# The order of the first loads and of the first TensorE work in a conditioned residual kernel

## Chip, cores and metric

The kernel runs on one core of one Trainium2 chip. The metric is the device time of one execution in microseconds (us); lower is better. A profiled execution gives the span from its first to its last instruction, and the time of the run lies a little above that span.

## What is computed

The batch has 128 samples, each a 128 x 1024 matrix of float32. Every sample picks one of 200 matrices for the first layer and one of 8 matrices and bias rows for the second.

```python
def _L0_cond_ref(x, conditions, weights):
    w = weights[conditions]
    return jnp.einsum('bct,bcd->bdt', x, w)

def _L1_cond_ref(x, subjects, weights, bias):
    w = weights[subjects]
    b = bias[subjects]
    out = jnp.einsum('bct,bcd->bdt', x, w)
    out = out + b[:, :, None]
    return out
x = x + _L0_cond_ref(x, itok_B_1_198, L0_cond_weights)
x = x + _L1_cond_ref(x, itok_B_0_7, L1_cond_weights, fside_8xS_0)
```

## The kernel before, in words

Both layers are folded into one matrix for each sample. With J = W1 + I (`j_all`, made once on VectorE at L348), the output is (W0 J + J) applied to x, plus the bias. So for each sample TensorE makes the 128 x 128 product W0 J (L291, in `product`), VectorE adds J to it and leaves M in `m_sb` (L374, in `sum_m`), and TensorE multiplies M with the two halves of x (L310, in `results`). VectorE takes the left half out of PSUM with the bias (L382), ScalarE the right half (L406), both in place into the x tile `xy`.

Samples go in pairs (1 MB of x), two pairs make a quad (2 MB), and `xy` holds a ring of eight pairs, four quads, so the 64 pairs take eight rounds. All large transfers are issued from SyncE (SP) in one written order: loads of x by pair (`load_pair`, L151) or by quad (`load_quad`, L148), loads of w0 of 64 KB for each sample (`load_one`, L129), and stores by pair (L166) or by quad (L162). A slot of the ring is loaded again only when its store has landed (L170). Transfers are issued in program order, and a wait on SP holds back everything behind it.

The w0 matrices stay in SBUF (`w0_home`), one place for each sample. In the first round every sample's matrix is loaded. From the second round on a sample whose matrix is already there skips its load; for this a table of homes is worked out in the prologue. TensorE spreads the 128 condition words over partitions (L316, L317), VectorE compares them in four steps (L353 to L360, each raises `home_step`), TensorE turns the resulting column into a row (L324, raises `home_turned`), and VectorE writes `load_words` and `pick_words` from it (L365, L367; four steps raise `home_ready`). SP waits for `home_ready` before the first load of the second round (L187), and GpSimd (POOL) before its picks of the second round (L272).

In the prologue SP issues `j_all` (L176), the two first pairs of x (L178, L179), waits for the condition words (L180, loaded from ScalarE's queue at L409), and then issues four w0 loads for each quad, with the next quad of x between them (L181 to L184). `load_w0_first` first reads four words into registers (L123) and then issues four transfers (L129). TensorE's queue holds the first product (L321), the turn of the table (L324), and then the alternation of results and products. The first product waits for the first pair's w0 (L285), and for POOL's copies of J (`picked`, L256, L258). VectorE's queue holds, in this order, the four comparing steps, two copies of words (L362, L363), the wait for `home_turned` (L364) with L365 and L367 behind it, and then the first sum (L386).

Of the kernel before, what the change touches and what calls it, by code (L numbers as in the profile page):

```python
# [11 lines left out]
def conditioned_residual_kernel(nc, x, cond, w0_t, w1_bias, out):  # L12
# [11 lines left out]
    NQ, C, QB, T = x.shape  # L24
    B = NQ * QB
    N0, _, D = w0_t.shape
    N1 = w1_bias.shape[1]
    assert C == D == 128
    PAIR = 2
    RING = 8  # L30
    QUAD = QB // PAIR
    QUADS = RING // QUAD
# [11 lines left out]
    with ExitStack() as ctx:  # L44
# [3 lines left out]
        def sem(name):  # L48
            return ctx.enter_context(nc.semaphore(name))
# [35 lines left out]
        pair_loaded = [sem(f"pair_loaded{s}") for s in range(QUAD)]  # L85
# [15 lines left out]
        def half(h):  # L101
            return slice(h * HALF, (h + 1) * HALF)

        def slots(q):
            return xy[:, q * QUAD:(q + 1) * QUAD, :, :].rearrange("c s k t -> c (s k t)")

        def quad_of(t, r, q):
            return t[bass.ds(r * QUADS + q, 1), :, :, :].rearrange("n c k t -> (n c) (k t)")

        def pair_of(t, n, s):  # L110
            return t[n, :, (s % QUAD) * PAIR:(s % QUAD + 1) * PAIR, :].rearrange("c k t -> c (k t)")
# [8 lines left out]
        def _(sp):  # L120
# [12 lines left out]
            def load_w0_first(q):  # L133
                words = words_of(cond_words[0:1, 0, q * QB:(q + 1) * QB])
                for k in range(QB):
                    load_one(q * QB + k, q * QUAD + k // PAIR, words[k], None)
# [10 lines left out]
            def load_quad(r, q):  # L147
                sp.dma_start(slots(q), quad_of(x, r, q)).then_inc(x_loaded[q], 16)  # L148

            def load_pair(n, s, loaded):  # L150
                sp.dma_start(xy[:, s, :, :].rearrange("c k t -> c (k t)"), pair_of(x, n, s)).then_inc(loaded, 16)  # L151
# [21 lines left out]
            def load_w0_of(r, q):  # L173
# [1 line left out]

            sp.dma_start(j_all[:].rearrange("c n d -> c (n d)"), w1_bias.rearrange("c n d -> c (n d)"))\  # L176
              .then_inc(w1_loaded, 16)
            for s in range(QUAD):  # L178
                load_pair(0, s, pair_loaded[s])  # L179
            sp.wait_ge(cond_loaded, 16)  # L180
            for q in range(QUADS):  # L181
                load_w0_first(q)
                if q < QUADS - 1:
                    load_quad(0, q + 1)  # L184


            sp.wait_ge(home_ready, 4)  # L187
# [42 lines left out]
        def _(pool):  # L230
            def pick(r, s):


                pool.wait_ge(w0_loaded[s], r * (PAIR * 16) + PAIR * 16)
                _, words = nc.values_load_multi_w_load_instructions(
                    pick_words[0:1, bass.ds(r * ROUND_B + s * PAIR, PAIR), :].rearrange("o b f -> o (b f)"),
                    engines=(mybir.EngineType.Pool,),
                    skip_runtime_bounds_check_because="each word is checked against its own range below")
                for k in range(PAIR):
                    home = nc.s_assert_within(words[2 * k], 0, B - 1)  # L240
                    i = nc.s_assert_within(words[2 * k + 1], 0, N1 - 1)
                    nc.gpsimd.tensor_copy(w0_pick[:, s, k, :],  # L242
                                          w0_home[:, bass.ds(home, 1), :].rearrange("k b c -> k (b c)"))
                    last = nc.gpsimd.tensor_copy(  # L244
                        j_pick[:, s, k, :], j_all[:, bass.ds(i, 1), :].rearrange("c n d -> c (n d)"))
                last.then_inc(picked, 1)

            def pick_first(s):


                _, words = nc.values_load_multi_w_load_instructions(
                    cond_words[0:1, 1, s * PAIR:(s + 1) * PAIR], engines=(mybir.EngineType.Pool,),
                    skip_runtime_bounds_check_because="each word is checked against its own range below")
                for k in range(PAIR):
                    i = nc.s_assert_within(words[k], 0, N1 - 1)
                    last = nc.gpsimd.tensor_copy(  # L256
                        j_pick[:, s, k, :], j_all[:, bass.ds(i, 1), :].rearrange("c n d -> c (n d)"))
                last.then_inc(picked, 1)  # L258
# [20 lines left out]
        @block.tensor  # L279
        def _(pe):  # L280
            def product(r, s, first=False):

                pe.wait_ge(picked, r * RING + (s + 1))
                if first:
                    pe.wait_ge(w0_loaded[s], PAIR * 16)  # L285
                if not first or s >= MB:

                    pe.wait_ge(m_ready[s % MB], r * (RING // MB) + s // MB)
                for k in range(PAIR):
                    w0_of_k = w0_home[:, s * PAIR + k, :] if first else w0_pick[:, s, k, :]  # L290
                    last = nc.tensor.matmul(m_ps[:, s % MB, k * D:(k + 1) * D], w0_of_k,  # L291
                                            j_pick[:, s, k, 0:D], start=True, stop=True)
                last.then_inc(product_ready, 1)

            def results(r, s, k, first=False, last=False):

                b = s * PAIR + k
                if k == 0:
                    if first and s < QUAD:
                        pe.wait_ge(pair_loaded[s], 16)  # L300
                    elif not last:
                        pe.wait_ge(x_loaded[s // QUAD], r * 16 + (16 if s >= QUAD else 0))
                    pe.wait_ge(m_ready[s % MB], r * (RING // MB) + (s // MB + 1))
                for h in range(2):
                    if last:
                        pe.wait_ge(last_x_loaded[2 * k + h], 16)
                    if not first or b >= YB:

                        pe.wait_ge((left_out, right_out)[h][b % YB], r * (ROUND_B // YB) + b // YB)
                    nc.tensor.matmul(y_ps[:, b % YB, h, :], m_sb[:, s, k, :], xy[:, s, k, half(h)],  # L310
                                     start=True, stop=True).then_inc(y_ready, 1)


            pe.wait_ge(ones_ready, 1)
            pe.wait_ge(cond0_row_ready, 1)
            nc.tensor.matmul(cond0_ps[:, 0:B], ones[:], cond0_row[:], start=True, stop=True)  # L316
            nc.tensor.matmul(cond0_ps[:, B:B + 1], cond0_row[:], ones[0:1, 0:1], start=True, stop=True)\  # L317
              .then_inc(cond0_spread, 1)


            product(0, 0, first=True)  # L321
            pe.wait_ge(eye_ready, 1)
            pe.wait_ge(home_step, 4)
            nc.tensor.matmul(home_ps[0:1, 0:B], home_less_b[:], eye[:], start=True, stop=True)\  # L324
              .then_inc(home_turned, 1)
            for s in range(1, RING):
                results(0, s - 1, 0, first=True)
                product(0, s, first=True)
                results(0, s - 1, 1, first=True)
            with pe.Fori(1, ROUNDS) as r:  # L330
                results(r - 1, LAST, 0)
                product(r, 0)
                results(r - 1, LAST, 1)
                for s in range(1, RING):
                    results(r, s - 1, 0)
                    product(r, s)
                    results(r, s - 1, 1)
            for k in range(PAIR):
                results(ROUNDS - 1, LAST, k, last=True)
# [110 lines left out]
```

## Time and profile before

| what | value |
|---|---|
| time, median of 3 runs | 342.62 us (342.51 to 342.78) |
| time of the profiled run | 343.0 us |
| its span | 341.2 us |
| TensorE matmul busy | 272.9 us (80%) |
| VectorE, ScalarE, GpSimd busy | 126.3, 97.0, 65.8 us |
| moved by DMA | 140.80 MB, mean 413 GB/s |
| share of SP's queue (q1) in 16 DMA engines' span | 98.7% |
| mean granted TensorE clock, of full speed | 0.952 |

The profiled run took 343.0 us, of which the span is 341.2 us, so 1.8 us lie around it; it is 0.4 us above the median. In the views below, times are counted from the span's start. PE is TensorE's matmul, PEld its weight load, DVE is VectorE, ACT ScalarE, POOL GpSimd, and SPq the queue of SyncE. The share of DMA is that of 16 DMA engines together, and since packets overlap, it can stand a little above 1.

### The profile page before, as it was taken

To read this page: it belongs to the slowest core of one execution; us is meant where nothing else is said; L and a number is where in the kernel's file an instruction comes from. 1 tells how busy PE (TensorE), PEld (TensorE's weight loads), DVE (VectorE), ACT (ScalarE), POOL (GpSimd) and SP (SyncE) were. 2 spreads that over 40 slices of the span, in tenths; PEclk is the share of its full clock that TensorE was granted. 3 is DMA by queue.
4 is the path that set the end of the run, shared out by engine and by line. 5 is a ranking of instruction groups with operands and counts; after the bars stand their busy time and mean duration, and the time that the engine had idled before them with its cause. 6 is when DMAs were issued, how large, how long until landed. Compare 5 with 4: busy or idle time off the path is not lost.

```text
span 341.2 us, 4867 instructions
## 1 busy us (share of the span) xinstructions
PE 272.9 (80%) x774; PEld 131.8 (39%) x774; DVE 126.3 (37%) x202; ACT 97.0 (28%) x135; POOL 65.8 (19%) x249
## 2 busy tenths in 40 slices
PE   1799997678777798786997977889697987978980
PEld 1355443334333354343443433444343443434430
DVE  3145543343333334243442433434243432424440
ACT  1033352232322224132241324313143321323330
POOL 2400311131122211222111222121222111222000
PEclk9999999999999979799897999979799997989996
DMA  7999999999999999999999999999999999999993
GB/s 304 417 409 396 422 430 419 413 423 421 432 434 423 426 422 414 431 424 423 427 427 423 431 430 426 427 421 426 433 426 430 427 429 426 425 426 424 413 387 137
DMA packets 24058, 140.80 MB, mean 413 GB/s; under 512 B 2673, under 2 KB 14322, under 8 KB 15474
## 3 DMA queue, kind: packets, MB, share of 16 engines
q1 hardware_dynamic: 23760, 140.20, 98.7%
q10 hardware_dynamic: 290, 0.53, 0.4%
q14 instruction: 7, 0.06, 0.0%
q8 instruction: 1, 0.02, 0.0%
HBM read 76.03 MB, written 67.11 MB: 419 GB/s over the span
## 4 chain that ended last, share of the span: by engine, by line
DMA 61%; SPq 16%; PE 13%; issue 7%; ACT 0%; DVE 0%; DVEq 0%
DMA out<-xy 54%; PE y_ps L310 11%; SPq L129 9%; SPq L123 5%; DMA xy<-x 4%; DMA w_home<-w_t 2%; PE m_ps L291 2%; SPq L148 2%; ACT xy L406 0%; SPq L162 0%; SPq L151 0%; SPq L203 0%; SPq L156 0%; PE home_ps L324 0%; SPq L176 0%
## 5 line engine op out<-in xcount | busy, mean ns | idle before, releaser
L310 PE MATMUL y_ps<-xy,m_sb 128*128 128x512 f32 x512 | 251.4, 627 | 49.2 <-DMA xy<-x 48.2
L310 PEld LDWEIGHTS y_ps<-xy,m_sb 128*128 128x128 f32 x512 | 94.6, 200 | 155.1 <-issue 155.1
L406 ACT ACTIVATE xy<-y_ps,j_pick 128x512 f32<-128x512 f32 x128 | 88.0, 687 | 227.4 <-PE y_ps L310 227.4
L382 DVE TENSOR_SCALAR xy<-y_ps,j_pick 128x512 f32<-128x512 f32 x128 | 96.1, 751 | 147.9 <-PE y_ps L310 147.9
L242 POOL COPY w_pick<-w_home 128x128 f32 x112 | 33.2, 296 | 238.3 <-issue 238.3
L291 PEld LDWEIGHTS m_ps<-j_pick,w_pick 128*128 128x128 f32 x224 | 35.7, 200 | 30.2 <-issue 29.7
L374 DVE TENSOR_TENSOR m_sb<-m_ps,j_pick 128x256 f32<-128x256 f32 x64 | 27.2, 425 | 47.7 <-PE m_ps L291 46.1
L291 PE MATMUL m_ps<-j_pick,w_pick 128*128 128x128 f32 x224 | 34.9, 279 | 0.0
L244 POOL COPY j_pick<-j_all 128x129 f32 x112 | 33.4, 298 | 0.1
L291 PE MATMUL m_ps<-j_pick,w_home 128*128 128x128 f32 x32 | 5.9, 315 | 6.6 <-DMA w_home<-w_t 6.6
L406 ACT ACT_TABLE_LOAD x7 | 9.0, 1283 | 7.5 <-POOL j_pick L256 7.4
L291 PEld LDWEIGHTS m_ps<-j_pick,w_home 128*128 128x128 f32 x32 | 5.7, 225 | 10.6 <-POOL j_pick L256 7.2
L256 POOL COPY j_pick<-j_all 128x129 f32 x16 | 4.8, 298 | 9.9 <-issue 9.5
L316 PE MATMUL cond_ps<-cond_row,ones 1*128 1x128 f32 x2 | 0.8, 482 | 2.4 <-DVE cond_row L345 2.4
L365 DVE TENSOR_TENSOR load_words<-home_ps,batch_less_b 1x128 int32<-1x128 f32 x1 | 0.3, 280 | 5.0 <-PE home_ps L324 5.0
L348 DVE TENSOR_TENSOR j_all<-j_all,eye 128x1024 f32<-128x1024 f32 x1 | 1.2, 1226 | 1.9 <-DMA j_all<-w_bias 1.9
L316 PEld LDWEIGHTS cond_ps<-cond_row,ones 1*128 1x128 f32 x2 | 0.5, 305 | 2.4 <-issue 2.4
L345 DVE CAST cond_row<-cond_words 1x128 f32<-1x128 int32 x1 | 0.2, 215 | 2.1 <-DMA cond_words<-cond 2.1
L324 PE MATMUL home_ps<-eye,home_less_b 128*1 128x128 f32 x2 | 0.6, 394 | 0.0
L317 PEld LDWEIGHTS cond_ps<-ones,cond_row 1*128 1x128 f32 x2 | 0.5, 328 | 0.0
L317 PE MATMUL cond_ps<-ones,cond_row 1*128 1x1 f32 x2 | 0.4, 277 | 0.0
L355 DVE TENSOR_SCALAR same<-cond_ps,cond_col 128x128 f32<-128x128 f32 x1 | 0.4, 351 | 0.0
(16 smaller groups left out, 2.8 us busy)
## 6 DMA issues: line engine op xcount, KB each, us to landing
xy<-x SPq DMA_DIRECT2D x30, 2048.0 KB, 15.1
out<-xy SPq DMA_DIRECT2D x29, 2048.0 KB, 15.0
w_home<-w_t SPq DMA_DIRECT2D x128, 64.0 KB
out<-xy SPq DMA_DIRECT2D x5, 1024.0 KB, 9.7
xy<-x SPq DMA_DIRECT2D x3, 1024.0 KB, 7.7
xy<-x SPq DMA_DIRECT2D x4, 256.0 KB, 13.4
j_all<-w_bias SPq DMA_DIRECT2D x1, 516.0 KB, 3.4
out<-xy SPq DMA_DIRECT2D x2, 256.0 KB, 4.7
```

Of the source, the lines that this page charges most:

```text
L123: return nc.values_load_multi_w_load_instructions(words, engines=(mybir.EngineType.SP,), min_val=0, max_val=N0 - 1, skip_runtime_bounds_ch ...
L129: sp.dma_start(w0_home[:, bass.ds(b, 1), :].rearrange("k b c -> k (b c)"), w0_t[bass.ds(i, 1), :, :].rearrange("n k c -> (n k) c"), cond=n ...
L148: sp.dma_start(slots(q), quad_of(x, r, q)).then_inc(x_loaded[q], 16)
L242: nc.gpsimd.tensor_copy(w0_pick[:, s, k, :], w0_home[:, bass.ds(home, 1), :].rearrange("k b c -> k (b c)"))
L244: last = nc.gpsimd.tensor_copy(j_pick[:, s, k, :], j_all[:, bass.ds(i, 1), :].rearrange("c n d -> c (n d)"))
L256: last = nc.gpsimd.tensor_copy(j_pick[:, s, k, :], j_all[:, bass.ds(i, 1), :].rearrange("c n d -> c (n d)"))
L291: last = nc.tensor.matmul(m_ps[:, s % MB, k * D:(k + 1) * D], w0_of_k, j_pick[:, s, k, 0:D], start=True, stop=True)
L310: nc.tensor.matmul(y_ps[:, b % YB, h, :], m_sb[:, s, k, :], xy[:, s, k, half(h)], start=True, stop=True).then_inc(y_ready, 1)
L316: nc.tensor.matmul(cond0_ps[:, 0:B], ones[:], cond0_row[:], start=True, stop=True)
L374: nc.vector.tensor_tensor(m_sb[:, s, :, :], m_ps[:, s % MB, 0:PAIR * D].rearrange("c (k d) -> c k d", k=PAIR), j_pick[:, s, :, 0:D], ALU.a ...
L382: nc.vector.tensor_scalar(xy[:, s, k, half(0)], y_ps[:, b % YB, 0, :], j_pick[:, s, k, D:D + 1], None, ALU.add).then_inc(left_out[b % YB], 1)
L406: nc.scalar.activation(xy[:, s, k, half(1)], y_ps[:, b % YB, 1, :], ACT.Identity, bias=j_pick[:, s, k, D:D + 1]).then_inc(right_out[b % YB ...
```

## The change

Two orders are changed in the prologue; no instruction is added or removed.

On SP, the first four w0 loads, with the wait for the condition words and the reading of the words, are moved from behind both first pairs of x to between them. The second pair follows them. From there the order of transfers is as before: quad 1, w0 of quad 1, quad 2, w0 of quad 2, quad 3, w0 of quad 3.

On TensorE, the turn of the table of homes with its two waits is moved ahead of the first product.

```diff
--- before.py
+++ after.py
@@ -175,13 +175,13 @@
 
             sp.dma_start(j_all[:].rearrange("c n d -> c (n d)"), w1_bias.rearrange("c n d -> c (n d)"))\
               .then_inc(w1_loaded, 16)
-            for s in range(QUAD):
-                load_pair(0, s, pair_loaded[s])
+            load_pair(0, 0, pair_loaded[0])
             sp.wait_ge(cond_loaded, 16)
-            for q in range(QUADS):
+            load_w0_first(0)
+            load_pair(0, 1, pair_loaded[1])
+            for q in range(1, QUADS):
+                load_quad(0, q)
                 load_w0_first(q)
-                if q < QUADS - 1:
-                    load_quad(0, q + 1)
 
 
             sp.wait_ge(home_ready, 4)
@@ -318,11 +318,11 @@
               .then_inc(cond0_spread, 1)
 
 
-            product(0, 0, first=True)
             pe.wait_ge(eye_ready, 1)
             pe.wait_ge(home_step, 4)
             nc.tensor.matmul(home_ps[0:1, 0:B], home_less_b[:], eye[:], start=True, stop=True)\
               .then_inc(home_turned, 1)
+            product(0, 0, first=True)
             for s in range(1, RING):
                 results(0, s - 1, 0, first=True)
                 product(0, s, first=True)
```

## Rows read from the trace of the kernel before

**Rows 1.** The page, part 2: DMA share in tenths and GB/s, 40 slices

```profile
DMA  7999999999999999999999999999999999999993
GB/s 304 417 409 396 422 430 419 413 423 421 432 434 423 426 422 414 431 424 423 427 427 423 431 430 426 427 421 426 433 426 430 427 429 426 425 426 424 413 387 137
```

**Rows 2.** Busy time by stretch, later stages; the columns stand in the first line

```profile
core 0: us, PE busy (x) PEld busy (x) DVE busy (x) ACT busy (x) POOL busy (x), PEclk, DMA share, GB/s
12.00:32.00 20.00, 19.27 (x51) 9.79 (x52) 8.29 (x15) 5.50 (x8) 2.09 (x7) 1.00 1.02 401
32.00:42.00 10.00, 10.00 (x33) 5.14 (x32) 5.03 (x9) 3.44 (x5) 3.21 (x12) 1.00 1.03 429
62.00:322.00 260.00, 213.82 (x607) 102.37 (x606) 96.58 (x151) 75.54 (x106) 53.53 (x200) 0.95 1.01 426
322.00:335.00 13.00, 8.91 (x24) 3.70 (x22) 4.35 (x7) 3.74 (x6) 0.00 (x0) 1.00 0.94 385
335.00:341.00 6.00, 0.00 (x0) 0.00 (x0) 0.00 (x0) 0.00 (x0) 0.00 (x0) 0.54 0.11 43
```

**Rows 3.** The same view, the first 7 us

```profile
1.80:2.00 0.20, 0.00 (x0) 0.00 (x0) 0.00 (x0) 0.00 (x0) 0.04 (x1) 1.00 2.01 227
2.00:7.00 5.00, 0.98 (x4) 0.92 (x4) 2.70 (x8) 0.00 (x0) 0.29 (x1) 1.00 0.96 383
```

**Rows 4.** The chain of waits in order of time: start, length, what

```profile
3.44 6.46 DMA w_home<-w_t
10.04 1.19 PE m_ps L291 x4
11.23 0.53 PE home_ps L324 x2
12.73 3.75 PE y_ps L310 x4
38.91 0.70 ACT xy L406
```

**Rows 5.** Timeline of SP's queue: start, length, engine, line, operation, tiles

```profile
0.79 0.39 SPq L176 DMA_DIRECT2D j_all<-w_bias  x1
1.23 0.89 SPq L151 DMA_DIRECT2D xy<-x  x2
2.88 2.16 SPq L129 DMA_DIRECT2D w_home<-w_t  x4
5.09 0.44 SPq L148 DMA_DIRECT2D xy<-x  x1
12.93 7.04 SPq L129 DMA_DIRECT2D w_home<-w_t  x6
20.70 0.35 SPq L166 DMA_DIRECT2D out<-xy  x1
28.05 4.22 SPq L166 DMA_DIRECT2D out<-xy  x2
```

**Rows 6.** Timeline of DVE and POOL ahead of the first product

```profile
2.09 0.21 DVE L345 CAST cond_row<-cond_words 1x128 f32<-1x128 int32 x1 [2.09 <-DMA cond_words<-cond]
6.20 0.29 DVE L360 TENSOR_REDUCE home_less_b<-same_batch 128x1 f32<-128x128 f32 x1
6.65 0.66 POOL L256 COPY j_pick<-j_all 128x129 f32 x2 [4.80 <-issue]
```

**Rows 7.** Issue to landing, in order: L176; L151, both first pairs

```profile
DMA to landing us min/median/max: 3.4/3.4/3.4
DMA to landing us min/median/max: 5.7/6.7/7.7
```

**Rows 8.** Issue to landing: L166 issued at 31.9; all L148; all L162

```profile
DMA to landing us min/median/max: 7.2/7.2/7.2
DMA to landing us min/median/max: 10.2/15.1/16.3
DMA to landing us min/median/max: 10.6/15.0/17.8
```

## The prediction

> **What bounds the kernel now.** I read the page's DMA line first. The 16 DMA engines are busy for nine tenths or more of every slice from the second to the last but one, and what they move hardly varies [rows 1]. TensorE is busy for 80% of the span, but in the long middle its matmuls fill 213.8 of 260 us while the DMA share is 1.01 at 426 GB/s [rows 2]. So the candidate is DMA, and the question for a change in the prologue is whether DMA ever runs dry between the first and the last byte. If it does not, work that is done earlier elsewhere buys nothing.
>
> The second view is busy time by stretch. From 2 to 7 us the share is 0.96 [rows 3], from 12 to 42 us it is 1.02 and 1.03 [rows 2]. It is idle only before 1.8 us [rows 3], and it thins out only after 335 us: 43 GB/s from 335 to 341 us with PE, DVE and ACT at zero [rows 2]. A sixteenth of 426 is 27 GB/s, so there some one or two of the 16 DMA engines work off what is left to them while all others are done. The last 6 us are therefore DMA too, the arrears of the slowest DMA engine, and not a computation that came late.
>
> The third view is the time from issue to landing. A quad of 2.1 MB takes 2.1/0.426 = 4.9 us to move, yet a quad's load needs at least 10.2 us from its issue and 15.1 at the median, a quad's store at least 10.6 and 15.0 [rows 8]. Even the shortest had some 5 us of other transfers ahead of it. The shallowest place in round 0 is the store of pair 3: its issue is the second of the two that start at 28.05, ends at 32.3 and so starts at 31.9 [rows 5], and it lands 7.2 us later [rows 8], against 1.05/0.426 = 2.5 us of its own. A backlog of over 4 us stands there as well.
>
> The chain of waits tells another story for the first 39 us: the landing of w0 at 3.44 + 6.46 = 9.90, then the product, the turn of the table, and TensorE without a break to 38.9 us [rows 4]. TensorE is on that chain because SP's stores wait for its results. But a chain names who came last at each wait, and not whether the queue behind it was empty. The landings say that it was not.
>
> **Part 1: w0 of the first four between the pairs.** Nothing is added. What moves on SP is the wait for the condition words, the reading of words, and four issues; what they are moved past is the issue of pair 1 alone.
>
> *When the w0 arrives.* Pair 0, issued at 1.23, lands 5.7 us later at 6.9; pair 1, issued at about 1.70 (the second of the row's two), lands 7.7 us later at 9.4 [rows 5, 7]. The four w0 land 0.5 us after it, at 9.9 [rows 4]. Without pair 1 ahead of them they land at 6.9 + 0.5 = 7.4, which is 2.5 us earlier, the time of one pair (1.05 MB at some 0.42 MB/us). They are in the queue in time: their issues start at 2.88 now [rows 5], behind the end of pair 1's issue at 2.12 and the reading of words. In the new order the SP is free at 1.65, but the condition words arrive only near 2.1 (VectorE, which waits for them too, starts at 2.09 [rows 6]), so the w0 issues move by 0.1 us at most.
>
> *What that does to pair 1.* It is issued where the four w0 issues end, 2.88 + 2.16 = 5.04 [rows 5], instead of 1.70. Pair 1 lands at 7.4 + 2.5 = 9.9, the time at which pair 1 and the four w0 are both there today. Its reader, the third and fourth result, comes after 13 us by the sum below, so nobody waits. Quad 1 and all behind it are issued one pair issue (0.42 us) later than now. By 7 us DMA has taken 0.05 + 5 x 0.383 = 1.96 MB [rows 3] of the 5.0 MB then issued, so this is hidden.
>
> *Does DMA run dry at 6 us?* This is the price that the trace of before does not show. Ahead of pair 1 stand j_all (0.53 MB), pair 0 (1.05) and four w0 (0.26), 1.84 MB. At 0.383 MB/us from 2 us, with 0.05 MB before it [rows 3], they last until 2 + 1.79/0.383 = 6.7 us. The nearest row for the start of a transfer is the first one: j_all is issued at 0.79 [rows 5] and data flow at 227 GB/s from 1.8 [rows 3], 1.0 us. That puts pair 1's first data at 6.0, with 0.7 us to spare, and the price at zero. The other end: j_all lands 3.4 us after its issue [rows 7], of which 0.53/0.40 = 1.3 is moving, so all fixed time together is 2.1 us. Were all of that before the first byte, data would come at 7.1 and DMA would be idle for 0.4 us. I take zero, since the row with the first data shows the start itself, and keep 0.4 us as the upper end.
>
> A rule of the Trainium skill speaks against the change here: "DMA: Bandwidth & Descriptors", section "Anatomy of one DMA", gives about 2.0 us of fixed time for each transfer beside bytes over 436 GB/s. By it j_all would need 3.2 us, and the trace has 3.4. Put wholly ahead of the data, it would leave DMA idle for 0.3 us. The page itself places most of it behind the last byte, which would leave nothing idle.
>
> **Part 2: the turn of the table ahead of the product.** Both waits of the turn are met early: the eye comes from POOL long before, and the last step of `home_step` ends at 6.20 + 0.29 = 6.49 [rows 6]. The turn (0.53 us [rows 4]) then runs from 6.6 to 7.2, inside the wait for the w0 of 7.4. It costs the product nothing. Were the w0 to land before 6.6, the product would wait for at most 0.6 us. What goes is the turn behind the product and the two VectorE steps ahead of the first sum (L365, L367): now the product ends at 11.23 and the first result starts at 12.73 [rows 4], 1.5 us later; afterwards only the sum and its hand-over are left, some 0.6 us.
>
> **The sum on TensorE.** Product from max(w0 7.4, first picks 6.65 + 0.66 = 7.3 [rows 6], turn 7.2) + 0.14 = 7.55; 1.19 us for the product [rows 4] gives 8.7; sum and hand-over 0.6; first result at 9.3 instead of 12.73. TensorE is 3.4 us ahead and stays so until the end of round 0 (38.9 becomes 35.5). POOL's picks come in time, and no x load is late for it: quad 1 lands at 5.09 + 10.2 = 15.3 [rows 5, 8], and its first reader comes behind pairs 0 and 1: at round 0's mean of 26.2/8 = 3.3 us a pair [rows 4], not before 9.3 + 6.5 = 15.8.
>
> **What is late next.** SP. Six w0 issues, from 12.93 on, take 7.04 us [rows 5] where four take 2.16: the queue is full and accepts a transfer only as fast as DMA drains. SP reaches the first store's wait at 20.0 whatever TensorE does, and issues it at 20.70, so of the 3.4 us this store sees at most 0.7. The later stores of round 0 may be issued up to 3.4 us earlier, but behind a backlog of over 4 us. They land when the bytes ahead of them have moved, in the same order as before. The first reload of a slot waits for such a landing, not for TensorE. There the 3.4 us end. From then on the order of transfers, their bytes, the start of the first and the fullness of the queue are as before, so the end is as before: 0 us, against the profiled run 341.2 in the span and 343.0 in all. The forecast is the median of the three runs, 342.6 us.
>
> **Rivals.**
> 1. *The start is on the path after all.* The chain has TensorE from 10 to 38.9 us [rows 4]. If DMA's share near 1 hid transfers that merely wait, each earlier store would bring the next load forward, and the gain would be up to 3.4 us: 339.2 us. The 401 GB/s between 12 and 32 us against 426 later [rows 2] speak for it a little: 20 us x 25/426 = 1.2 us are lost there. Against it stand the landings [rows 8] and the many short w0 rows in that stretch. Chance 0.07. Half of the 1.2 us, 0.6, is the lower end that I allow to the forecast.
> 2. *A gap at 6 us, slower.* If pair 1's first data come later than 6.7 us, DMA stands idle, and a queue that never runs dry later cannot make it up: each 0.1 us of gap is 0.1 us at the end. It shows as slower from a gap of 0.7 us on, that is, if the first data come 2.4 us after the issue at 5.0. At 0.8 us the time is 343.4. The start of 1.0 us [rows 3, 5] speaks against it; the w0 issues at 0.54 us each, slower than DMA moves them, speak for it. Chance 0.06.
> 3. *The order does not do what it says.* The w0 may still land near 9.9, if the small transfers are held up behind something else than pair 1. Then only the turn is gained on TensorE, 0.9 us, and the time is again 342.6. Chance 0.03.
>
> **How the numbers follow.** The forecast has 0.84. About 0.2% (0.7 us) is what a measurement of this kernel can tell from no change. The forecast and rival 3 both lie within it: same 0.87. Rival 1 is faster, 0.07; rival 2 is slower, 0.06. The forecast's own bounds are 342.6 - 0.6 and 342.6 + 0.4, with 0.2 for the scatter of the runs on the upper side, and as it holds over 8 in 10, the range reaches to no other case: 342.0 to 343.2.
>
> **What the profile afterwards would show.** First product near 7.5 and first result near 9.3 us; pair 1 landing near 9.9 and quad 1 near 15.3, as before; the DMA share between 5 and 8 us near 1 (a hole there is rival 2); the first store of SP near 20; the first reload at the same time as before, within half a microsecond; TensorE through round 0 near 35.5; and the stretch 335 to 341 as it was. The prediction is wrong if the first reload comes over 1 us earlier and the span shrinks with it, or if the DMA is found dry.

## The result, and the profile after

| | before | changed |
|---|---|---|
| median of 12 runs each | 342.62 us (342.15 to 343.54) | 343.99 us (342.99 to 345.33) |
| ratio | | 1.0038, 95% interval 1.0023 to 1.0052 |
| profiled run, its span | 343.0, 341.2 us | 344.31, 342.5 us |

The change makes the kernel slower by 1.3 us, 0.38%. Two further comparisons of the same kernel gave 1.0021 (1.0007 to 1.0036) and 1.0029 (1.0019 to 1.0040), so 0.7 to 1.3 us by the ratios. The forecast was no change.

The page of the changed kernel, part 2, in the lines that answer to [rows 1]:

```profile
DMA  7999999999999999999999999999999999999985
GB/s 257 411 416 383 416 382 421 413 415 429 427 429 423 421 421 432 423 427 420 424 427 423 434 434 417 428 418 427 436 419 429 436 433 412 441 429 418 421 357 214
```

The first slice holds 257 GB/s instead of 304. The slice from 42.8 to 51.4 us is low too, 382 instead of 430. The others look much as before, up to the last two. Busy time by stretch, against [rows 2] (engines' busy us, granted clock, DMA share, GB/s):

```profile
12.00:32.00 20.00, 19.09 (x57) 9.71 (x56) 8.70 (x14) 6.18 (x9) 2.37 (x8) 1.00 1.02 398
...
42.00:52.00 10.00, 5.76 (x13) 2.53 (x12) 2.16 (x4) 2.66 (x3) 2.12 (x8) 0.83 1.01 389
...
62.00:322.00 260.00, 208.56 (x603) 100.63 (x602) 96.55 (x151) 75.12 (x105) 54.23 (x204) 0.97 1.01 425
322.00:335.00 13.00, 11.78 (x34) 5.46 (x32) 5.86 (x9) 4.81 (x7) 0.00 (x0) 1.00 0.90 379
335.00:341.00 6.00, 0.00 (x0) 0.00 (x0) 0.00 (x0) 0.00 (x0) 0.00 (x0) 0.81 0.60 229
```

The long middle is as before, 425 GB/s against 426. The last stretch now carries 229 GB/s where it had 43: bytes that were not moved earlier are moved here. They are (229 - 43) x 6 us = 1.1 MB, more than one hole at the start accounts for. Most of them belong to two stretches. One is the hole between 5.5 and 8 us, which the rest of this section and most experiments are about. The other lies at 42 to 52 us, where the kernel before has

```profile
42.00:52.00 10.00, 10.00 (x30) 4.88 (x29) 5.13 (x8) 4.72 (x6) 1.07 (x4) 1.00 1.01 422
```

There the changed kernel moves 389 GB/s, which is (422 - 389) x 10/426 = 0.8 us of transfer, and TensorE is busy for 5.76 us instead of 10, since it waits for x. It comes back in "Why the prediction was wrong". The first hole is seen in the same view in steps of half a microsecond, of the changed kernel:

```profile
5.00:5.50 0.50, 0.00 (x0) 0.00 (x0) 0.50 (x1) 0.00 (x0) 0.00 (x0) 1.00 1.04 426
5.50:6.00 0.50, 0.00 (x0) 0.00 (x0) 0.47 (x3) 0.00 (x0) 0.00 (x0) 1.00 0.81 331
6.00:6.50 0.50, 0.00 (x0) 0.00 (x0) 0.47 (x2) 0.00 (x0) 0.00 (x0) 1.00 0.83 270
6.50:7.00 0.50, 0.00 (x0) 0.00 (x0) 0.47 (x3) 0.00 (x0) 0.00 (x0) 1.00 0.60 160
7.00:7.50 0.50, 0.39 (x2) 0.11 (x2) 0.22 (x2) 0.00 (x0) 0.31 (x2) 1.00 0.51 140
7.50:8.00 0.50, 0.36 (x2) 0.17 (x2) 0.27 (x2) 0.12 (x1) 0.28 (x1) 1.00 0.95 310
8.00:8.50 0.50, 0.50 (x3) 0.50 (x4) 0.21 (x2) 0.50 (x1) 0.11 (x1) 1.00 1.04 420
2.00:12.00 10.00, 5.05 (x13) 3.14 (x14) 3.77 (x12) 1.28 (x1) 2.35 (x8) 1.00 0.94 361
```

and of the kernel before:

```profile
6.50:7.00 0.50, 0.00 (x0) 0.00 (x0) 0.25 (x2) 0.00 (x0) 0.29 (x1) 1.00 0.93 393
7.00:7.50 0.50, 0.00 (x0) 0.00 (x0) 0.00 (x0) 0.10 (x1) 0.30 (x1) 1.00 1.01 426
2.00:12.00 10.00, 2.68 (x10) 1.93 (x10) 2.92 (x10) 1.28 (x1) 2.68 (x9) 1.00 1.02 407
```

From 5.5 to 8 us the rates are 331, 270, 160, 140 and 310, a mean of 242 GB/s. Against 426 that is 2.5 x (1 - 242/426) = 1.1 us of lost transfer. Over 2 to 12 us it is 361 against 407 GB/s, (407 - 361) x 10/426 = 1.1 us again. It is the rate that shows the hole, and not the share: at 6.0 to 6.5 us the share is still 0.83 with 270 GB/s. What came before the hole is in the timeline of SP's queue (start, length, what), against [rows 5]:

```profile
3.65 1.97 SPq L129 DMA_DIRECT2D w_home<-w_t  x4
5.67 0.42 SPq L151 DMA_DIRECT2D xy<-x  x1
6.15 0.42 SPq L148 DMA_DIRECT2D xy<-x  x1
...
23.50 0.34 SPq L166 DMA_DIRECT2D out<-xy  x1
...
36.95 0.34 SPq L148 DMA_DIRECT2D xy<-x  x1
```

Pair 1 is issued at 5.67 instead of 1.70. The forecast had 5.04. The 0.6 us between are the condition words, as the start of the chain of waits shows:

```profile
0.79 2.15 DMA cond_words<-cond
...
2.96 0.51 SPq L123
```

The loss then stays. SP's last reload of a quad is issued at 299.92 in the trace of before and 1.4 us later in this one, and the spans differ by 1.3 us:

```profile
301.31 0.34 SPq L148 DMA_DIRECT2D xy<-x  x1
```

TensorE's part went nearly as forecast. Its timeline has the turn, the first product and the first result, and ScalarE's has the 12th output of the round (L406) at 36.74:

```profile
7.11 0.58 PE L323 MATMUL home_ps<-eye,home_less_b 128*1 128x128 f32 x2 [2.81 <-DVE home_less_b L360]
...
7.83 1.23 PE L291 MATMUL m_ps<-j_pick,w_home 128*128 128x128 f32 x4
...
9.73 1.19 PE L310 MATMUL y_ps<-xy,m_sb 128*128 128x512 f32 x1 [0.68 <-DVE m_sb L374]
```

The first result starts at 9.73 instead of 12.73 and buys nothing: the first store goes out at 23.50 instead of 20.70, and the first reload of a slot at 36.95 instead of 33.85. SP itself is late by then: the w0 loads of quad 1 take 3.54 us to issue instead of 1.93, quad 2 is issued at 10.69 instead of 8.02, and the last six w0 start at 16.02 instead of 12.93.

### The profile page after: what moved, and what is told of

The parts are those of the page before. It is cut to its first block, busy times and chain, and to the rows that moved or that the text cites. A ratio compares the mean times of both kernels' runs of the same rounds, so it can differ in the third digit from the quotient of the medians.

```text
span 342.5 us, 4867 instructions
## 1 busy us (share of the span) xinstructions
PE 269.7 (79%) x774; PEld 131.1 (38%) x774; DVE 126.4 (37%) x202; ACT 96.9 (28%) x135; POOL 65.3 (19%) x249
## 4 chain that ended last, share of the span: by engine, by line
DMA 62%; SPq 20%; PE 8%; issue 7%; ACT 0%
DMA out<-xy 53%; SPq L129 12%; DMA xy<-x 9%; PE y_ps L310 7%; SPq L123 5%; SPq L148 2%; PE m_ps L291 1%; DMA cond_words<-cond 1%; ACT xy L406 0%; SPq L162 0%; SPq L156 0%; SPq L203 0%; SPq L151 0%; SPq L157 0%; SPq L166 0%
## 5 line engine op out<-in xcount | busy, mean ns | idle before, releaser
L310 PE MATMUL y_ps<-xy,m_sb 128*128 128x512 f32 x512 | 247.2, 619 | 56.9 <-DMA xy<-x 56.2
L406 ACT ACTIVATE xy<-y_ps,j_pick 128x512 f32<-128x512 f32 x128 | 87.9, 687 | 229.6 <-PE y_ps L310 229.6
L291 PE MATMUL m_ps<-j_pick,w_pick 128*128 128x128 f32 x224 | 35.9, 285 | 0.0
```

The costliest lines, as they stand in the source:

```text
L406: nc.scalar.activation(xy[:, s, k, half(1)], y_ps[:, b % YB, 1, :], ACT.Identity, bias=j_pick[:, s, k, D:D + 1]).then_inc(right_out[b % YB ...
```

## The experiments

Times are medians of runs taken beside runs of the kernel before on the same chip. Three questions are asked: is it SP's order or TensorE's; is it the hole in DMA or the small transfers among the large; and is the hole made by the late words alone. The expectations name theories by letters. G: the gap in the stream of DMA makes the loss. T: TensorE's new order or earlier work does. S: the small w0 transfers between the large ones do. I: TensorE's early start adds a loss of its own to the gap. W: the condition words are late because of SP's order. C: they are late by chance.

| kernel | words land, us | DMA 2 to 12 us, GB/s | last reload, us | span of the trace, us | ratio, interval |
|---|---|---|---|---|---|
| before | 2.1 | 407 | 299.92 | 341.2 | |
| before_r2 | 2.1 | 410 | 299.78 | 341.1 | single run |
| part2 | 2.1 | 405 | 299.38 | 340.6 | 1.0008 (0.9995 to 1.0022) |
| no_cond | 2.1 | 403 | 299.22 | 340.2 | 0.9995 (0.9978 to 1.0012) |
| two_w0 | 2.1 | 392 | 299.41 | 340.7 | 1.0002 (0.9983 to 1.0021) |
| two_w0_r2 | 2.1 | 398 | 299.19 | 340.4 | 1.0003 (0.9989 to 1.0017) |
| filled | 3.0 | 384 | 299.75 | 341.0 | 1.0002 (0.9990 to 1.0013) |
| part1 | 3.1 | 361 | 300.39 | 341.6 | 1.0017 (1.0005 to 1.0029) |
| gap_only | 2.2 | 354 | 300.70 | 341.9 | 1.0049 (1.0035 to 1.0062) |
| changed | 3.0 | 361 | 301.31 | 342.5 | 1.0038 (1.0023 to 1.0052) |
| after_again | 3.1 | 349 | 299.98 | 341.2 | 1.0021 (1.0007 to 1.0036) |
| after_r3 | 2.1 | 360 | 300.74 | 342.1 | 1.0029 (1.0019 to 1.0040) |
| after_r4 | 3.0 | 356 | 301.37 | 342.7 | single run |

The words' column is the start of VectorE's first instruction, which waits for them.

**part1: SP's order alone.**

```diff
-            for s in range(QUAD):
-                load_pair(0, s, pair_loaded[s])
+            load_pair(0, 0, pair_loaded[0])
             sp.wait_ge(cond_loaded, 16)
...
+            load_w0_first(0)
+            load_pair(0, 1, pair_loaded[1])
...
```

> Only the order of SP is changed (the four w0 between the first two pairs of x); TensorE's queue is as before. Theory G (gap): the changed kernel's trace shows DMA at 215 and 225 GB/s from 6 to 8 us, since pair 1 is issued only behind the condition words and four w0 issues; that idle time reaches the end. Then this kernel costs all of the change's loss: about 343.7 to 344.2 us, ratio near 1.004. Theory T (TensorE's turn or its earlier work does harm): this kernel is less than half of the loss, 342.6 to 343.2.

Measured: 343.31 beside 342.81 us, 0.17%. It is clearly above before. It lies between the two forecasts (T up to 343.2, G from 343.7), and 0.17% is less than half of the 0.38% of the first comparison, so this run by itself decides for neither; gap_only, filled and no_cond do. The hole is there:

```profile
6.00:7.00 1.00, 0.00 (x0) 0.00 (x0) 0.90 (x5) 0.00 (x0) 0.13 (x1) 1.00 0.76 223
7.00:8.00 1.00, 0.42 (x2) 0.42 (x3) 0.00 (x0) 0.38 (x1) 0.46 (x2) 1.00 0.77 165
```

**part2: TensorE's order alone.**

```diff
-            product(0, 0, first=True)
             pe.wait_ge(eye_ready, 1)
...
+            product(0, 0, first=True)
```

> Only TensorE's queue is changed (turn of the table ahead of the first product); SP's order is as before. Theory G: no DMA is moved and none runs dry, 342.6 us, ratio 1.000. Theory T: it carries half or more of the loss, 343.3 us or more.

Measured: 342.88 beside 342.81 us; the interval holds 1. That is near theory G's value, and below T's bound. The turn's move costs nothing that could be measured.

**gap_only: a hole and nothing else.**

```diff
-            for s in range(QUAD):
-                load_pair(0, s, pair_loaded[s])
+            load_pair(0, 0, pair_loaded[0])
+            sp.wait_ge(home_step, 1)
+            load_pair(0, 1, pair_loaded[1])
```

> The order of transfers and TensorE's queue are those of before; only pair 1 is held back on SP until VectorE has done its first comparing step (about 5.4 us instead of 1.7), with nothing in its place. Ahead of pair 1 stand j_all and pair 0 alone, 1.57 MB, gone at about 5.8 us, and pair 1's data can come at 6.5 to 7.3. Theory G: DMA idles 0.7 to 1.5 us and the end is later by as much: 343.3 to 344.1 us. Theory S (the loss is the stall of a single DMA engine in the 512-byte rows of w0, seen in the changed kernel's late last increments, and idle time as such is made up elsewhere): 342.6 us, as the w0 rows are queued between large transfers again.

Measured, in five runs: 344.42 beside 342.81 us, 0.49%, the largest loss of all, though no transfer changed its place and TensorE's queue is untouched. It is more than theory G had named (344.1 at most). Theory S, as put here, is out: no w0 stands ahead of pair 1. The trace, in the view of before:

```profile
5.50:6.00 0.50, 0.00 (x0) 0.00 (x0) 0.47 (x2) 0.00 (x0) 0.00 (x0) 1.00 0.70 295
6.00:6.50 0.50, 0.00 (x0) 0.00 (x0) 0.47 (x4) 0.00 (x0) 0.00 (x0) 1.00 0.67 131
6.50:7.00 0.50, 0.00 (x0) 0.00 (x0) 0.16 (x2) 0.00 (x0) 0.38 (x2) 1.00 0.90 147
7.00:7.50 0.50, 0.00 (x0) 0.00 (x0) 0.00 (x0) 0.19 (x1) 0.21 (x1) 1.00 0.76 213
7.50:8.00 0.50, 0.00 (x0) 0.00 (x0) 0.00 (x0) 0.50 (x1) 0.18 (x1) 1.00 0.82 344
2.00:12.00 10.00, 1.90 (x8) 1.85 (x8) 2.69 (x8) 1.28 (x1) 2.69 (x10) 1.00 0.96 354
```

The time from issue to landing of its pair 1:

```profile
DMA to landing us min/median/max: 5.1/5.1/5.1
```

Pair 1 is issued at 5.4 and DMA is back above 300 GB/s only from 7.5. It lands 5.1 us after its issue, and moving 1.05 MB takes 2.5 us of that. Between issue and a strong stream stand about 2 us. The 1.0 us of the prediction is the time to the first packets (147 GB/s from 6.5).

**filled: half of pair 1 ahead of the wait.**

```diff
             load_pair(0, 0, pair_loaded[0])
+            sp.dma_start(xy[:, 1, 0, :], x[0, :, 2, :]).then_inc(pair_loaded[1], 16)
             sp.wait_ge(cond_loaded, 16)
             load_w0_first(0)
-            load_pair(0, 1, pair_loaded[1])
+            sp.dma_start(xy[:, 1, 1, :], x[0, :, 3, :]).then_inc(pair_loaded[1], 16)
...
```

(TensorE's wait for that pair is raised to 32, for both halves.)

> As the changed kernel, but the first sample of pair 1 (0.5 MB) is issued ahead of the wait for the condition words and its second sample behind the four w0, so that 0.5 MB more, 1.2 us of DMA time, stand in the queue meanwhile. Theory G: the gap of about 1.1 us is filled, no stretch of 1 us under 350 GB/s between 3 and 12 us, and the time is before's, 342.6 to 342.9 us (rows of 4 KB for 1 MB may cost 0.1 us). Theory S: w0 ahead of x data does the harm by itself, and the time stays near 344.0. Theory T: also near 344.0, since TensorE's order and its early start are the changed kernel's.

Measured: 342.96 beside 342.81 us, ratio 1.0002. The time is theory G's. Its words about the trace were not quite met: the microsecond from 7 to 8 has 297 GB/s, so a dent is left. TensorE's order and w0 ahead of the second half of pair 1 are the changed kernel's, and the loss is gone. So is the lateness of SP as a cause: the words came at 3.0 here as well, and quad 1 is issued at 6.24, as late as in the changed kernel (6.15).

**no_cond: the changed order without its wait.**

```diff
-            sp.wait_ge(cond_loaded, 16)
-            load_w0_first(0)
+            for k in range(QB):
+                sp.dma_start(w0_home[:, k, :], w0_t[k, :, :]).then_inc(w0_loaded[k // PAIR], 16)
             load_pair(0, 1, pair_loaded[1])
...
```

> As the changed kernel, but the first four w0 loads take fixed table rows 0 to 3 and so wait for no condition words and read none; the wait stands behind quad 1. (This leaves out the choice of w0 for the first four samples, so their results are not the reference's.) Pair 1 is then issued near 3.4 us instead of 5.67. Theory G: j_all and pair 0 last until 5.8 us, no hole at 6 to 8 us, and the time is before's, 342.6 to 342.9 us, although w0 stands ahead of pair 1 and TensorE starts 3 us early. Theory S (the 512-byte rows between pairs do harm by themselves) and theory I: 343.5 us or more.

Measured: 342.50 beside 342.70 us, ratio 0.9995. SP issues pair 1 at 3.9 here, and the stream holds:

```profile
1.70 2.16 SPq L180 DMA_DIRECT2D w_home<-w_t  x4
3.91 0.45 SPq L151 DMA_DIRECT2D xy<-x  x1
```

```profile
6.00:6.50 0.50, 0.00 (x0) 0.00 (x0) 0.47 (x2) 0.00 (x0) 0.00 (x0) 1.00 0.98 333
...
7.00:7.50 0.50, 0.43 (x2) 0.11 (x2) 0.18 (x2) 0.00 (x0) 0.35 (x2) 1.00 1.32 496
2.00:12.00 10.00, 5.10 (x13) 3.14 (x14) 3.82 (x12) 1.28 (x1) 2.35 (x8) 1.00 1.03 403
```

This is the cleanest pair with the changed kernel: the same order of transfers and the same queue of TensorE, and the loss goes with the wait. It also answers what an early TensorE is worth when nothing is lost for it: nothing that can be told from no change (0.9978 to 1.0012).

**two_w0 and two_w0_r2: two w0 ahead of pair 1 instead of four.**

```diff
-            load_w0_first(0)
+            words = words_of(cond_words[0:1, 0, 0:QB])
+            for k in range(PAIR):
+                load_one(k, 0, words[k], None)
             load_pair(0, 1, pair_loaded[1])
+            for k in range(PAIR, QB):
+                load_one(k, 1, words[k], None)
```

> As the changed kernel, but only the w0 of the first pair (two of the four) stands ahead of pair 1, the other two behind it. Pair 1 is issued 1.1 us earlier. Theory G: the hole shrinks from about 1.1 us to between 0.2 and 0.5 us, and the time lies between before's and the changed kernel's, 342.8 to 343.2 us. Theory S: w0 ahead of x does harm by its presence, near the changed kernel's time.

> The order with only two w0 ahead of pair 1, again. Its median was 342.48 beside 342.70, with an interval of 0.9983 to 1.0021. If this order is worth something, it should repeat at 0.999 or below; by theory G it should not gain, since DMA has no idle time left to win: ratio 1.000, within 0.9985 to 1.0015. Theory W has its condition words at 2.1 us again (and then needs a reason why this order differs from the changed one, whose instructions up to that wait are the same); theory C allows 3.0.

Measured: 342.48 beside 342.70 us (1.0002), and 343.08 beside 342.74 us (1.0003). The words came at 2.1 in both, so pair 1 was issued at 3.72 and 3.76, some 1.9 us before that of the changed kernel and not 1.1. Theory G's price for a smaller hole was a miss: 392 and 398 GB/s from 2 to 12 us are (408 - 395) x 10/426 = 0.3 us of transfer less than before's two traces, and no loss was measured. The low first median did not repeat, so this order is no gain either.

**after_again, after_r3, after_r4, before_r2: the two kernels again.** No edit.

> The changed kernel once more, beside the others of this call. The SP order alone gave a ratio of 1.0017 (1.0005 to 1.0029), the whole change 1.0038 (1.0023 to 1.0052) on another chip. Theory G (the gap is all of it): the whole change is here too at 1.001 to 1.003. Theory I (TensorE's early start adds a loss of its own once w0 is early): 1.003 or more. In its trace the condition words should again come at 2.9 to 3.1 us if SP's order is what delays them, at 2.1 if that was chance.

> The changed kernel a third time, for its ratio and for two things that one trace can't tell. Theory W (the words are late because of SP's order): VectorE, which waits for the condition words, starts at 2.9 to 3.1 us here too, as in both earlier traces of this kernel. Theory C (chance, an execution in which that one small transfer is slow): 2.1 us in at least one of the three further traces of this order in this call. Time by theory G: before's low times plus 0.5 to 1.1 us, ratio 1.001 to 1.003.

> The changed kernel a fourth time, one look. Theory W: the condition words near 3.0 us. Theory C: 2.1 us here or in its twin. Whichever it is, the bytes moved from 2 to 12 us should follow it: with words at 3.0 some 350 to 360 GB/s, with words at 2.1 some 385 or more.

> The kernel before, a second look. Theory W: the condition words at 2.1 us, as in its first trace. Theory C: it may be either. Even late words (3.0) would cost it nothing, since pair 1 and with it 2.5 us of DMA time are in the queue ahead of them: 400 to 410 GB/s from 2 to 12 us in either case.

Measured: 343.26 beside 342.70 us; 343.91 beside 342.74 us; single runs of 344.47 and 342.87 us. Theory I had asked for 1.003 or more; 1.0021 and 1.0029 are below that and the first 1.0038 above. The three lie above the 1.0017 of SP's part alone, but the intervals overlap, so an added loss is neither shown nor excluded. Theory W is out as it was put. The words came at 3.0 in three of four traces of this kernel, and at 2.1 in the fourth, as in both of two_w0. after_r3, the timeline of VectorE's first step and of SP, and then the rates:

```profile
2.07 0.21 DVE L345 CAST cond_row<-cond_words 1x128 f32<-1x128 int32 x1 [2.07 <-DMA cond_words<-cond]
...
2.75 2.03 SPq L129 DMA_DIRECT2D w_home<-w_t  x4
...
4.84 0.42 SPq L151 DMA_DIRECT2D xy<-x  x1
```

```profile
5.50:6.00 0.50, 0.00 (x0) 0.00 (x0) 0.47 (x3) 0.00 (x0) 0.00 (x0) 1.00 0.79 326
6.00:6.50 0.50, 0.00 (x0) 0.00 (x0) 0.47 (x2) 0.00 (x0) 0.00 (x0) 1.00 1.00 321
6.50:7.00 0.50, 0.00 (x0) 0.00 (x0) 0.47 (x4) 0.00 (x0) 0.00 (x0) 1.00 0.79 232
7.00:7.50 0.50, 0.44 (x2) 0.11 (x2) 0.17 (x2) 0.00 (x0) 0.36 (x2) 1.00 0.73 226
7.50:8.00 0.50, 0.37 (x2) 0.22 (x2) 0.31 (x2) 0.17 (x1) 0.23 (x1) 1.00 0.76 217
2.00:12.00 10.00, 5.10 (x13) 3.14 (x14) 3.83 (x12) 1.28 (x1) 2.35 (x8) 1.00 0.98 360
```

With the words in time, pair 1 is issued at 4.84, the 5.04 of the prediction and a bit earlier, and the hole is there all the same: 360 GB/s from 2 to 12 us, a mean of 264 from 5.5 to 8. after_r4 had late words and 356, against the expectation that the bytes follow the words. So the late words make SP late, and the hole comes without them too. What runs in it can be seen from the packets that start in a half microsecond, here 6.5 to 7 and 7 to 7.5 us of after_r3, and then 6.5 to 7 us of no_cond:

```profile
DMA packets 245, 0.12 MB, mean 232 GB/s; under 512 B 34, under 2 KB 244, under 8 KB 244
DMA packets 80, 0.11 MB, mean 226 GB/s; under 512 B 9, under 2 KB 70, under 8 KB 70
```

```profile
DMA packets 275, 0.19 MB, mean 382 GB/s; under 512 B 37, under 2 KB 266, under 8 KB 266
```

Nearly all of them are the 512-byte rows of the four w0. In after_r3 the four are issued by 4.8 us, yet their rows run from 6.0 to 7.5, one large packet beside 244 small ones from 6.5 to 7, and pair 1's packets come behind them. In no_cond, where pair 1 is issued 0.9 us earlier, 9 large packets run beside 266 small ones, and 25 beside 98 in the next half microsecond (496 GB/s).

**relieve: who sets the last 6 us.**

```diff
-            store_quad(ROUNDS - 1, 0)
+            wait_out(ROUNDS - 1, QUAD - 1)
+            for rows in (slice(0, 120), slice(120, 128)):
+                sp.dma_start(quad_of(out, ROUNDS - 1, 0)[rows, :], slots(0)[rows, :]).then_inc(stored[0], 16)
```

(The final wait on that semaphore is raised by 16.)

> The kernel before, with one of its last stores (quad 0 of the last round) cut into rows 0 to 119 and rows 120 to 127. It asks who sets the last 6 us. A section of the Trainium skill's page 'DMA: Bandwidth & Descriptors' (on why a DMA increments its semaphore by 16) says that a transfer of 120 rows runs on the 15 lowest-numbered DMA engines and one of 8 rows on the 8 lowest; the last engine would then be spared 8 rows. From rows: a row of a quad takes one engine 16 KB / (426/16 GB/s) = 0.62 us, so an engine that is left out is spared 8 x 0.62 = 4.9 us, and the first eight get one row more, 0.6 us. If the engine in arrears at the end is the one left out, the 6 us at 43 GB/s shrink to 1 or 2 and the time is 338 to 340 us. If it is another, or no engine is left out, 342.6 to 343.2 us.

Measured: 344.23 beside 342.70 us, ratio 1.0043 (1.0030 to 1.0056). Neither forecast was met. The end, in the view of [rows 2]:

```profile
335.00:341.00 6.00, 0.00 (x0) 0.00 (x0) 0.00 (x0) 0.00 (x0) 0.00 (x0) 0.52 0.56 221
```

The last stretch carries 221 GB/s, so the work of all engines ends later, and whether the one in arrears was spared can't be read. No view gives the bytes of single DMA engines either, so it isn't shown that the pieces ran on 15 and on 8 of them. What the trace does show is a hole of its own: from 313 to 322 us DMA moves 288 GB/s, against 420 in the trace of before, 9 x (420 - 288)/426 = 2.8 us of transfer, while SP needs 7.40 us to issue the four last loads instead of 2.75. Why the two pieces lead to that was not followed up. That a single DMA engine is in arrears remains a reading of the 43 GB/s, and which one it is stays open.

## Why the prediction was wrong, by its own steps

*What bounds the kernel: held.* DMA never ran dry in before, and the converse was shown by gap_only: time that DMA loses at 6 us is missing at the end. Against the first trace of before, the last reload and the span are later together, by 0.5 and 0.4 us in part1, 0.8 and 0.7 in gap_only, 1.4 and 1.3 in the changed kernel.

*An early TensorE is worth nothing that could be measured: held* (no_cond, filled, two_w0). The forecast of its times was near: turn 7.1 (forecast 6.6), product 7.83 (7.55), first result 9.73 (9.3). One row was misread. The 38.9 of [rows 4] is not the end of round 0 but the 12th of its 16 outputs, the one that the store of quad 2 waits for, so a pair takes 3.9 us and not 3.3. That output now starts at 36.74, 2.2 us earlier instead of 3.4, since quad 1 came late: issued at 6.15 it landed 12.1 us later, at 18.3, and not at 15.3 as before. The issues behind pair 1 were forecast 0.42 us later than before; quad 1 is 1.1 and quad 2 2.7 us later. The forecast of no change did not hang on either: filled has quad 1 as late and no loss.

*"Does DMA run dry at 6 us": the step that failed.* It was priced at zero with an upper end of 0.4 us, and it is 1.1 us of transfer. Two terms of it were off, and a third lay beside them.

- Issue to data was taken as 1.0 us and as the start of a full stream. About 1 us is right for the first packets, but the rate then climbs for another microsecond or more: in gap_only pair 1 is issued at 5.4 and DMA is above 300 GB/s from 7.5, in the changed kernel 5.67 and 7.5, in after_r3 4.84 and only 8.0 (217 GB/s before it, 330 from there). The trace of before had this in its first transfer, issued at 0.79; the mean of 383 GB/s over 2 to 7 us hid it:

```profile
2.00:2.50 0.50, 0.05 (x1) 0.08 (x1) 0.21 (x1) 0.00 (x0) 0.00 (x0) 1.00 0.54 157
2.50:3.00 0.50, 0.50 (x2) 0.50 (x3) 0.00 (x0) 0.00 (x0) 0.00 (x0) 1.00 0.92 372
```

  The prediction's own upper end, 2.1 us, was near the right value; it was laid aside because the other row seemed to show the start itself. The Trainium skill ("DMA: Bandwidth & Descriptors", section "Anatomy of one DMA") gives 2.0 us of fixed time, for transfers issued from GpSimd, while these come from SyncE. The size is near what is left here beside moving, 2.1 us for j_all and 2.6 for pair 1 of gap_only, but these traces show a good part of it ahead of the stream, where the page has most of it behind the last byte.
- The four w0 were counted as 0.26 MB of cover at the full rate. The rate falls at 5.5 us and not at 6.7, as j_all and pair 0 (1.58 MB) run out: in the changed kernel the half-microsecond rates up to 5.5 add up to 1.37 MB, up to 6.0 to 1.54. Behind them the rows of w0 run nearly alone, at 232 to 321 GB/s in after_r3 and 160 to 270 in the changed kernel. The prediction named the pace of the w0 issues (0.54 us each) as what speaks for rival 2 and did not put it into the sum. That pace can't be the whole of it: in after_r3 the four are issued by 4.8, before any of their rows run. Where pair 1 was issued 2 us and more before j_all and pair 0 ended, near 6.0 (no_cond 3.91, two_w0 3.72), there is no hole or a small one; with 1.2 us (after_r3) the hole is whole. Why small rows alone move less was not tested.
- The condition words were taken to come at 2.1 us, from one execution. In the orders that wait for them before pair 1 is complete they came at 3.0 in five of eight traces, in the other orders in none of six; whether the order has a part in that stays open, since the same kernel showed both. Late words move SP by 0.9 us, but after_r3 shows that the hole does not need them.

*Rival 2 was the right one, at 0.06 far too small a chance.* Its mechanism is what happened, and its price of 0.8 us lies inside what the three comparisons gave. Its conversion of 0.1 us to 0.1 us holds only roughly: the holes of the changed kernel (1.1 to 1.4 us of transfer), of part1 (1.1) and of gap_only (1.3) cost 0.7 to 1.3, 0.6 and 1.6 to 1.7 us, and in the one trace of after_again the hole is the deepest while its last reload (299.98) and span (341.2) are before's. Small holes were free: two_w0 and filled moved 0.3 and 0.6 us less by 12 us and lost nothing that was measured.

Two things in the traces narrow this down. The first is the second loss, at 42 to 52 us: 389 GB/s in the first trace of the changed kernel and 396 in after_r4, against 413 in after_r3, 419 in after_again, 421 in part1 and 417 in gap_only. The second is what reaches the end. By the mean rate over the first 52 us (397 GB/s in before), the four traces of the changed kernel are behind by 2.3, 1.2 (after_again), 1.6 (after_r3) and 1.8 us (after_r4) of transfer, part1 by 1.0, gap_only by 1.1, filled by 0.4. Their spans are later by 1.3, 0.0, 0.9, 1.5, 0.4, 0.7 and -0.2 us. So 0.3 to 1.2 us of each lag does not reach the end, and the rest does. The stretch of 43 GB/s at the end, where most of DMA has nothing left to do, is a place that can take it up; that it does so was not tested, and executions of one kernel differ by 1 to 2 us. The second loss may be part of why the first comparison gave 1.3 us and part1 0.6. It was seen clearly only in two traces of the changed kernel, where TensorE starts early and then waits for x (4.2 us in the first), and what makes it stays open.

*The range* was cut at 343.2 with 0.4 us for a hole whose two ends had been worked out from one row each. With the large transfers alone as the cover (until 2 + 1.53/0.383 = 6.0) and data at 7.1 the upper end is 1.1 us, and the range would have reached 344.

## What to carry to other kernels

In a kernel that DMA bounds from the first byte to the last, a new order in the prologue can let the stream of DMA thin out, and every wait that is moved ahead of a large issue has to be priced by the work then queued. Count the large transfers as that work, and the small ones for less than their bytes, and have the next large transfer issued some 2 us before the ones ahead of it end. Take the start of a stream from rates in half-microsecond steps, not from a mean or from the first packets. Where a wait must stand early, put something large in front of it that doesn't depend on it: filled has w0 early and lost nothing that was measured.

## What the runs showed of the hardware that was not expected

- A 1 MB transfer issued at 5.4 us, when j_all and pair 0 were nearly through (gap_only), found DMA at 147 GB/s from 6.5 to 7, 213 to 7.5 and 344 to 8, and landed 5.1 us after its issue, twice the 2.5 us that it takes to move.
- The 1 KB of condition words, issued at 0.79 in every kernel, landed at 2.1 us or at 3.0 us, with nothing between in 14 traces (2.07 to 2.17, and 2.96 to 3.09). The same kernel showed both.
- The 512-byte rows of four w0 transfers, with almost no large packet beside them, ran at 232 GB/s (after_r3, 6.5 to 7 us); with large packets beside as many of them, DMA moved 382 GB/s (no_cond, the same half microsecond).
- A store of 2 MB in rows 0 to 119 and 120 to 127 instead of 128 cost 1.5 us, 0.43%, near the end of this kernel.
